# Transposing six of eight activation chunks by DMA instead of on TensorE, between the second layer norm and the feed-forward

## The reference, cut to what matters

```
x = layernorm(x + attn(x))            # x: (4, 2048, 2048)
x = layernorm(x + ffn(x))

attn: q = x@Wq; v = x@Wv; states = decayed running sum of v over the sequence
      y = layernorm(q * states) * ln_g + ln_b
      return (y * silu(x@Wg)) @ Wo
ffn:  gate, up = split(x @ w_gate_up.T)      # 2 x 8192 wide
      return (silu(gate) * up) @ w_down.T
```

## Time and profile before

| | |
|---|---|
| median of 3 runs | 2276.4 us (2271.61 to 2277.75) |
| the profiled execution | 2271.24 us |
| its span on core 1, the slowest | 2269.6 us (the 8 cores: 2260.5 to 2269.6) |
| TensorE busy in the span | 1917.1 us (84%) |
| VectorE, ScalarE, GpSimd busy | 577.8, 343.1, 110.2 us |
| mean granted TensorE clock | 0.922 on core 1 |

### The profile page before, as it was taken

How to read it: one execution, slowest core, us unless ns; L and a number is a source line. 1 busy time by engine, 2 the same in 40 slices (tenths; PEclk the granted TensorE clock), 3 DMA queues, 4 the chain that set the end, 5 groups by cost and what they waited for, 6 DMA issues and landing times.

```text
span 2269.6 us, 25399 instructions; the slowest of 8 cores (2260.5 to 2269.6 us)
## 1 busy us (share of the span) xinstructions
PE 1917.1 (84%) x9898; PEld 968.3 (43%) x9898; DVE 577.8 (25%) x1351; ACT 343.1 (15%) x402; POOL 110.2 (5%) x230
## 2 busy tenths in 40 slices
PE   4898999931676469999999999999999999997760
PEld 2346864400554334444444444444444444443320
DVE  4212234578315430001111111111111111111164
ACT  0100015400000102222112112112112112110002
POOL 1000000000000000000000000000000000000000
PEclk8999999955888769999999999999999999998985
DMA  8651334330042033436444435435435435422223
GB/s 121 121 93 26 69 57 75 65 84 0 1 76 79 32 56 75 75 75 112 75 74 81 80 63 93 75 56 93 75 58 96 80 60 97 75 46 47 38 37 148
DMA packets 32453, 161.04 MB, mean 71 GB/s; under 512 B 3668, under 2 KB 3668, under 8 KB 22100
## 3 DMA queue, kind: packets, MB, share of 16 engines
q0 software_dynamic: 29744, 142.62, 35.7%
q1 hardware_dynamic: 2596, 16.79, 1.9%
HBM read 293.62 MB, written 8.39 MB: 133 GB/s over the span
## 4 chain that ended last, share of the span: by engine, by line
PE 79%; DVE 10%; DMA 5%; issue 3%; ACT 2%; DVEq 0%; POOL 0%; ACTq 0%; POOLq 0%; SPq 0%
PE p L1075 20%; PE p L1106 19%; PE p L1169 18%; PE p L492 5%; PE p L590 5%; PE p L966 5%; PE p L370 4%; DMA warena<-wd_t 2%; DMA bbuf<-x_loc 2%; DMA warena<-wo 1%; DVE sqscr L790 1%; DVE sqscr L788 1%; DVE qbuf L797 1%; DVE mscr L1010 1%; DVE sqscr L792 1%
## 5 line engine op out<-in xcount | busy, mean ns | idle before, releaser
L1075 PE MATMUL p<-tbuf,warena 128*128 128x512 bf16 x2048 | 464.7, 380 | 7.9 <-DMA warena<-wgu_t 7.9
L1106 PE MATMUL p<-tbuf,warena 128*128 128x512 bf16 x2048 | 462.9, 379 | 0.0
L1093 ACT ACT_TABLE_LOAD x128 | 164.2, 1283 | 1015.4 <-PE p L1075 1015.4
L1075 PEld LDWEIGHTS p<-tbuf,warena 128*128 128x128 bf16 x2048 | 200.7, 98 | 250.9 <-issue 10.5
L1106 PEld LDWEIGHTS p<-tbuf,warena 128*128 128x128 bf16 x2048 | 200.4, 98 | 241.6
L1169 PE MATMUL p<-warena,vbuf 128*128 128x512 bf16 x1024 | 232.0, 389 | 43.9 <-DMA warena<-wd_t 36.7
L966 PE MATMUL p<-warena,qbuf 128*128 128x256 bf16 x1024 | 152.5, 298 | 136.3 <-DVE bbuf L980 78.9
L1169 PE MATMUL p<-warena,qbuf 128*128 128x512 bf16 x1024 | 222.3, 379 | 0.0
L966 PEld LDWEIGHTS p<-warena,qbuf 128*128 128x128 bf16 x1024 | 107.6, 105 | 182.5 <-issue 150.6
L1185 DVE TENSOR_TENSOR bbuf<-bbuf,p 128x512 bf16<-128x512 bf16 x128 | 87.9, 687 | 380.7 <-PE p L1169 380.7
L1169 PEld LDWEIGHTS p<-warena,vbuf 128*128 128x128 bf16 x1024 | 101.3, 100 | 173.9 <-issue 60.4
(11 more groups left out here) (125 smaller groups left out, 730.0 us busy)
## 6 DMA issues: line engine op xcount, KB each, us to landing
warena<-wgu_t POOLq DMA_DIRECT2D x128, 512.0 KB, 7.9
warena<-wd_t POOLq DMA_DIRECT2D x32, 1024.0 KB, 14.2
warena<-wq POOLq DMA_DIRECT2D x8, 1024.0 KB, 9.5
warena<-wv POOLq DMA_DIRECT2D x8, 1024.0 KB, 9.8
warena<-wg POOLq DMA_DIRECT2D x8, 1024.0 KB, 9.0
warena<-wo POOLq DMA_DIRECT2D x8, 1024.0 KB, 18.4
sscr<-x_loc SPq DMA_DIRECT2D x8, 1024.0 KB, 5.6
out_loc<-sscr SPq DMA_DIRECT2D x8, 1024.0 KB, 4.2
```

Source lines behind the costliest of these rows:

```text
L1075: inst = t.matmul(p[gbk][:, 0:NT], warena[:, (j % 2) * GUSL + k * OPW + ot * 128: (j % 2) * GUSL + k * OPW + (ot + 1) * 128], tbuf[:, k * ...
L1093: inst = sc.activation(sscr[:, SIL_OFF + (gg % 2) * NT: SIL_OFF + (gg % 2 + 1) * NT], p[gbk][:, 0:NT], AF.Silu)
L1106: inst = t.matmul(p[ubk][:, 0:NT], warena[:, (2 + j % 2) * GUSL + k * OPW + ot * 128: (2 + j % 2) * GUSL + k * OPW + (ot + 1) * 128], tbuf ...
```

## The change

For chunks 0 to 5 (`ci < NCH - 2`) the TensorE transposes and VectorE copies are replaced by 16 DMA transposes each, issued by ScalarE, from `bbuf` to `tbuf`, one for each 128x128 block. ScalarE waits for the chunk's normalisation, and ahead of the first also for the last gate matmul (the last reader of the old `tbuf`). Chunks 6 and 7 are transposed as before; which of the two banks they use and for what they wait is now kept in a list. The first matmul of the feed-forward waits for all DMA transposes as well.

```diff
+        if ci < NCH - 2 and KT >= 8:
+            @blk.scalar
+            def _(sc, ci=ci):
+                if ci == 0:
+                    sc.wait_ge(sT, mil[("gpdone", NPAN - 1)])
+                sc.wait_ge(sV, mil[("l2nm", ci)])
+                for dt in range(KT):
+                    mil[("l2tx", ci)] = dtick(sc.dma_start(
+                        tbuf[:, dt * TOK + ci * 128: dt * TOK + (ci + 1) * 128],
+                        bbuf[:, ci * D + dt * 128: ci * D + (dt + 1) * 128],
+                        transpose=True), "xt2")
+            return
+
         for g2 in range(ntg):
-            gpar = (ci * ntg + g2) % 2
+            idx0 = len(l2t_hist)
+            gpar = idx0 % 2
+            l2t_hist.append((ci, g2))
...
-                idx = ci * ntg + g2
-                if idx >= 2:
-                    t.wait_ge(sV, mil[("l2tev", idx - 2)])
+                if idx0 >= 2:
+                    t.wait_ge(sV, mil[("l2tev", l2t_hist[idx0 - 2])])
...
     mil["x2T_done"] = cnt["V"]
+    mil["x2T_dma"] = ("xt2", ds["xt2"][1])
...
                         if j == 0:
                             t.wait_ge(sV, mil["x2T_done"])
+                            dwait(t, mil["x2T_dma"])
```

More of the change, by code:

```diff
@@ L122, in build_program @@
     ds = {}
-    for dn in ["small", "x", "xh0", "xh1", "xld0", "xld1", "w0", "w1", "w2", "w3",
+    for dn in ["xt2", "small", "x", "xh0", "xh1", "xld0", "xld1", "w0", "w1", "w2", "w3",
                "gu0", "gu1", "gu2", "gu3", "wd0", "wd1", "out0", "out1"]:
@@ L879, in build_program @@
     ntg = (KT + 7) // 8
+    l2t_hist = []
     def emit_ln2C(ci):
@@ L892, in _ @@
             mil[("l2nm", ci)] = tick(inst, "V")
+        if ci < NCH - 2 and KT >= 8:
[10 more added lines that the diff above has]
+            return
         for g2 in range(ntg):
-            gpar = (ci * ntg + g2) % 2
+            idx0 = len(l2t_hist)
+            gpar = idx0 % 2
+            l2t_hist.append((ci, g2))
             @blk.tensor
-            def _(t, ci=ci, g2=g2, gpar=gpar):
+            def _(t, ci=ci, g2=g2, gpar=gpar, idx0=idx0):
                 if g2 == 0:
                     t.wait_ge(sV, mil[("l2nm", ci)])
-                idx = ci * ntg + g2
-                if idx >= 2:
-                    t.wait_ge(sV, mil[("l2tev", idx - 2)])
+                if idx0 >= 2:
+                    t.wait_ge(sV, mil[("l2tev", l2t_hist[idx0 - 2])])
                 else:
@@ L915, in _ @@
                                        ident[:, :])
-                mil[("l2tr", ci * ntg + g2)] = tick(inst, "T")
+                mil[("l2tr", ci, g2)] = tick(inst, "T")
             @blk.vector
             def _(v, ci=ci, g2=g2, gpar=gpar):
-                v.wait_ge(sT, mil[("l2tr", ci * ntg + g2)])
+                v.wait_ge(sT, mil[("l2tr", ci, g2)])
                 bank = tp_bank(gpar)
@@ L929, in _ @@
                         bank[:, j * 128:(j + 1) * 128])
-                mil[("l2tev", ci * ntg + g2)] = tick(inst, "V")
+                mil[("l2tev", (ci, g2))] = tick(inst, "V")
     wo_banks = [4, 5]
```

## The result

The changed kernel takes 2363.99 us (median of 10 runs) against 2276.14 us (10 runs of the kernel before): +87.9 us. The ratio is 1.0391, 95% interval 1.0379 to 1.0402. The forecast was 2351.5 us, slower, with a range of 2273 to 2400 us. Every ratio here leaves out the executions in which some cores ran at a lower granted clock and took longer (3 of the 10 before, 2 of the 10 after), while the medians are of all runs; by the others alone the growth is 88 to 89 us.

What follows compares the result with a forecast made beforehand. TensorE bounds the kernel, so a later first feed-forward matmul moves the end equally. Rounds removed, -20.9 us, and the DMA chain, +101.2 us, gave +80.3 us on 2271.2 us: 2351.5 us, range 2273 to 2400 us.

Steps and rivals of the forecast that it cites:

- The place and the bound: Hole before the feed-forward: TensorE and VectorE finish near 800 us, weight loads are covered, DMA into tbuf releases the first matmul.
- The sign that was named for the queue: In the profile after, an issue record itself 1.2 us long would mean the queue, not the landing, sets the pace.
- The 20.9 us: Before the feed-forward: six 4.29 us rounds removed (25.7 us), six normalisations kept (4.8 us); the largest possible gain.
- The pace t: Time from one DMA transpose to the next on ScalarE's queue, taken as 1.24 us, middle of 0.38 and 2.1 us.
- First issue: Start of the DMA transposes, once chunk 0 is normalised, forecast at 786.6 us.
- last landing: End of the DMA chain: 2.1 us from the last transpose's issue to its landing.
- landing to matmul: From the last landing to the first feed-forward matmul, forecast as 0.4 us (0.38 from the trace).
- The estimate from the Trainium skill: Alternative price of 1.309 us per DMA transpose on ScalarE's queue, giving a shift of +86.9 us.
- Rival 1, a wash: ScalarE's queue handles a transpose as a copy, 0.33 to 0.41 us each: 2265.1 to 2272.7 us; chance 0.11.
- Rival 2: ScalarE's queue takes a transpose in under 0.18 us, feed-forward starts at 805.7 us: 2250.3 us; chance 0.05.
- Rival 3: A transpose's issue on ScalarE's queue is double a copy's, 0.47 to 0.8 us: 2278 to 2310 us; chance 0.20.
- Rival 4: Each DMA transpose waits for the one before, 1.7 to 2.1 us or above: 2395 to 2433 us and beyond; chance 0.12.

## Why the prediction was right

- **The place and the bound.** As forecast, TensorE and VectorE finish near 800 us, the weight loads are issued at 800.82 us and covered, and the first matmul is released by the DMA into tbuf. The sign that was named for the queue came too: the issue record itself is 1.2 us long. The shift arrives at the end undiminished: 87.85 us at the first matmul, 88 to 89 us in the runs. The 20.9 us taken off VectorE and TensorE were real and hidden.
- **The pace t, the one disputed term.** I took 1.24 us, the middle between the issue of a copy and a transpose that waits for its landing. On core 3 the pace is (912.89 - 789.62)/95 = 1.298 us: 1.233 us of issue and 0.03 us between, and some 3 us more for issues of up to 2.5 us early on. That is 5.5 us more than forecast over 95 steps. That 1.24 us was nearly right is luck: it was the mean of two mechanisms, and both were wrong. The landing is not part of it at all; the issue alone is 1.2 us, even for the first one into an empty queue (1.18 to 1.20 us on the eight cores).
- **The other terms.** First issue 789.62 instead of 786.6 us on core 3 (+3.0), last landing 2.40 instead of 2.1 us (+0.3), landing to matmul 0.24 instead of 0.38 us. 906.9 + 3.0 + 5.5 + 0.3 - 0.1 = 915.6 us, where the trace has 915.53. As means over the cores the account is simpler. The first issue is at 786.65 us, as forecast, the pace is 1.299 us (+5.6 us), and the forecast counted from the 826.58 us of core 1, 1.6 us later than the mean: 80.3 + 5.6 + 1.6 + 0.3 for the rest gives 87.8 us of the 87.85.
- **The estimate from the Trainium skill.** The Trainium skill (VectorE: DVE Perf Modes, "The three transpose paths") has 1309 ns for the DMA transpose. The trace has 1233 to 1265 ns of issue and a mean pace of 1299 ns, and the estimate of +86.9 us made from that figure was within 1 us of the result. The Trainium skill does not say whether its figure is a pace in a row of transposes, so the closeness may be partly luck.
- **Rival 1, a wash.** Fell: no issue of a transpose is below 1.08 us, on either queue and at either size. It was also priced too low: copies cost +29.8 us and not nothing. The Trainium skill (Advanced Engine Details and Errata, "X-Bar Transpose (TRN2)") says that transposes are as fast as ordinary DMAs. That does not hold here for the issue of 128x128 blocks: on odd cores 1.23 us against 0.61 us for a copy of the same block, on even cores 1.27 against 0.62 us. It may hold for the bytes, which set no pace in any run here.
- **Rival 2, faster.** Fell with rival 1.
- **Rival 3, a small loss.** Its factor held and its base did not. A transpose takes twice the issue of a copy, but a copy from SBUF takes 0.61 to 0.62 us and not 0.33 us, so the doubled price is 1.23 to 1.27 us; the forecast of rival 3 (0.47 to 0.8 us) fell. Whether the cause of the factor is two passes, no run shows.
- **Rival 4, serial.** Fell: a landing takes 2.4 us, a new transpose is issued every 1.26 to 1.3 us.

Shown: the price goes with the number of instructions (48, 96, 192), not with their number of partitions (64 or 128), not with the queue (ScalarE or SP), and it is the transposition that doubles it. Open: what the queue does in those 1.2 us, and whether a larger block would be had for the same price; 128x128 is the largest tried here.

## What to carry to other kernels

Price DMAs in a chain by the count of instructions times the issue time on their queue before looking at bytes: 96 transposes of 32 KB cost 124 us of issue while the DMA engines were 12% busy. In these runs a DMA transpose was free only where its queue had nothing else to do and nobody waited for its end (16 beside other work cost nothing, 96 on the path cost 88 us). And look at what stage a wait belongs to: four more PSUM banks in the stage ahead gave 37 us, where moving the transposes alone gave 2 to 6 us.

## What the runs showed of the hardware that I had not expected

- Odd and even cores differ steadily, in every run: 1.233 and 1.265 us (medians) for a transpose issued by ScalarE, 1.202 and 1.232 us by SP, 0.607 and 0.622 us for a copy from SBUF by ScalarE. For a copy from HBM they are alike, 0.451 and 0.453 us. No run here tells why.
- The price of a transpose does not fall with the block: 1.26 us (even cores) for 64x128 as for 128x128.
- A plain DMA of 128 rows of 256 bytes costs its queue 0.33 to 0.38 us at the head of a run and 0.45 us further on when it reads HBM (ScalarE's queue), 0.47 to 0.52 us for the first and 0.59 to 0.62 us further on when it reads SBUF (either queue).
- On seven cores of one run the only issue above 1.4 us (it takes 1.8 to 2.4 us) falls together with the only packet of the instruction queue q8; the eighth core has neither.
